# A sequence layer with routed experts on one core: TensorE transposes the identity where it would wait, and ScalarE takes the next group's first layer norm

## The reference, cut to what matters

```python
x = x + attn(_layernorm(x))      # in-projection, conv over 4 taps, damped oscillator scan, gate, out-projection
x = x + ffn(_layernorm(x))       # shared expert + 8 routed experts (top 2), exact gelu
def _layernorm(x, axis=-1, eps=1e-05):
    m = jnp.mean(x, axis=axis, keepdims=True)
    v = jnp.var(x, axis=axis, keepdims=True)
    return (x - m) / jnp.sqrt(v + eps)
# the scan, per head (64 wide, state 128):
v = (v - dt*A*y + dt*u*Bv) / denom;   y = y + dt*v + dt*u*By;   o = y.Cy + v.Cv
```

## Time and profile before

| | us |
|---|---|
| median of 3 runs (lowest, highest) | 561.17 (560.84, 562.13) |
| the profiled execution, its device time | 566.59 |
| its span, first to last instruction | 564.9 |
| PE busy | 456.9 (81%) |
| DVE busy | 454.3 (80%) |
| POOL busy | 283.8 (50%) |
| ACT busy | 238.8 (42%) |
| granted TensorE clock, mean | 0.921 |

### The profile page before, as it was taken

One profiled execution on the slowest core, in us unless ns is written; L12 is line 12 of the kernel. 1 busy time (PEld: TensorE's weight loads), 2 busy tenths in 40 slices (PEclk: granted clock), 3 DMA queues, 4 the chain that ended last, 5 costly groups with the idle time before them and its releaser, 6 DMA issues.

```text
span 564.9 us, 9434 instructions
## 1 busy us (share of the span) xinstructions
PE 456.9 (81%) x3163; PEld 352.7 (62%) x3163; DVE 454.3 (80%) x1280; ACT 238.8 (42%) x470; POOL 283.8 (50%) x361
## 2 busy tenths in 40 slices
PE   5882249993989959896689959898498996998997
PEld 4361248762856658674566747766385675786886
DVE  6599998968689997968689997977868987788542
ACT  1423225444275424443356523533437542443463
POOL 2007866666108855657305756576601785767100
PEclk9997569999899978999799995999899997998999
DMA  7400000200000010200000000020000000000000
GB/s 226 139 0 1 1 1 2 76 2 0 1 1 1 1 38 1 67 11 1 1 1 1 1 20 0 2 77 2 1 0 0 2 1 20 1 2 1 2 11 9
DMA packets 14793, 10.22 MB, mean 18 GB/s; under 512 B 1797, under 2 KB 13966, under 8 KB 14618
## 3 DMA queue, kind: packets, MB, share of 16 engines
q1 hardware_dynamic: 14746, 9.63, 5.9%
HBM read 8.55 MB, written 1.07 MB: 17 GB/s over the span
## 4 chain that ended last, share of the span: by engine, by line
DVE 37%; PE 36%; POOL 13%; issue 8%; ACT 4%; DMA 0%; SPq 0%; DVEq 0%; POOLq 0%; ACTq 0%
DVE tpA L1263 5%; PE BC L609 5%; DVE GV L1263 5%; DVE xr L1411 5%; PE HB L512 4%; POOL vt L1590 4%; PE HB L501 3%; DVE BC L1274 3%; POOL rinv L1625 3%; PE GV L631 3%; PE HB L569 3%; PE RR L667 2%; PE OO L684 2%; POOL big L1587 2%; DVE GV L1274 2%
## 5 line engine op out<-in xcount | busy, mean ns | idle before, releaser
L609 PE MATMUL BC<-xnT,winT 128*128 128x128 f32 x512 | 80.9, 309 | 44.2 <-DVE mm L1311 22.4
L609 PEld LDWEIGHTS BC<-xnT,winT 128*128 128x128 f32 x512 | 71.3, 216 | 57.4 <-issue 29.5
L1587 POOL TENSOR_TENSOR big<-mm 128x256 f32<-128x256 f32 x64 | 50.3, 785 | 74.7 <-DVE mm L1311 74.7
L1610 POOL TENSOR_SCALAR uT<-uT,skipT 128x512 f32<-128x512 f32 x8 | 12.5, 1570 | 95.4 <-DVE w L1396 55.5
L631 PE MATMUL GV<-big,vt 128*128 128x128 f32 x256 | 45.5, 305 | 17.6 <-POOL vt L1590 17.6
L1590 POOL TENSOR_TENSOR vt<-mm 128x256 f32<-128x256 f32 x64 | 58.5, 914 | 0.0
L561 PE MATMUL HB<-xnT,w 128*128 128x512 f32 x108 | 52.0, 603 | 3.7 <-ACT gtm L988 2.1
L631 PEld LDWEIGHTS GV<-big,vt 128*128 128x128 f32 x256 | 37.4, 210 | 23.4 <-POOL vt L1590 21.1
L1309 DVE TENSOR_TENSOR mm<-BC,pr 128x512 f32<-128x512 f32 x64 | 44.2, 691 | 6.0 <-DVE BC L1291 0.5
L925 ACT ACTIVATE big<-GV 128x256 f32<-128x256 f32 x60 | 23.0, 383 | 61.3 <-PE GV L634 59.6
L1599 POOL TENSOR_TENSOR mm<-ab,pr 128x256 f32<-128x256 f32 x48 | 41.4, 885 | 13.9 <-ACT pr L903 13.9
(11 more groups left out here) (208 smaller groups left out, 1133.8 us busy)
## 6 DMA issues: line engine op xcount, KB each, us to landing
ab<-dt_rows SPq DMA_DIRECT2D x12, 256.0 KB, 4.2
xr<-in_x SPq DMA_DIRECT2D x4, 256.0 KB, 5.1
winT<-in_w_inT SPq DMA_DIRECT2D x1, 1024.0 KB, 7.0
w<-in_rw SPq DMA_DIRECT2D x1, 1024.0 KB
out<-xr SPq DMA_DIRECT2D x3, 256.0 KB, 2.3
taps<-in_dw_wT SPq DMA_DIRECT2D x1, 512.0 KB, 3.7
w<-in_sw SPq DMA_DIRECT2D x2, 128.0 KB
out<-xr SPq DMA_DIRECT2D x2, 128.0 KB, 1.8
```

Of the source, the lines that this page charges most:

```text
L609: last = pe.matmul(b[:, j * TS:(j + 1) * TS], winT[:, col:col + NS], xt, start=True, stop=True)
L1587: pool.tensor_tensor(wt[q % 8][:], m[:, 0], m[:, 3], ALU.add)
```

## The change: what it does

Three things. `keep_busy` writes the HB bank that comes next instead of GV1, and therefore waits for the same read as that bank's next user. It is called in more places: more of them at the start (22, 3 and 15 for 10, 1 and 7); 5 after each of steps 14 to 31 of group 0; 3 after each of the first seven fills of every group and 4 more once DVE has scaled pair 0 (`first_pairs`, which also holds the two projections that open a group); 5 in `tail` of a group's last tile between its two products, 7 at the head of `op` of that tile, and 5 ahead of the second layer norm's transpose, for groups 0 to 2. And the first layer norm of groups 1 to 3 is applied by ACT (`Identity` with a scale and a bias, after pair 3's square and pair 1's copy) instead of DVE, for which POOL works out `shift` = -mean x rstd with two more small instructions.

```diff
-WARM = (10, 1, 7)
+WARM = (22, 3, 15)
+IDLE_STEP, PER_STEP, PER_FILL, AT_FIRST_PAIR = 14, 5, 3, 4
+AT_TAIL, AT_OUT, AT_NORM = 5, 7, 5
...
             def norm_T(kind, g):
+                if kind == LN2 and whole(g):
+                    keep_busy(AT_NORM)
                 pe.wait_ge(ln_xn, ln_index(kind, g) + 1)
...
             def keep_busy(n):
 
+                free = uses[0]
+                if free >= 2:
+                    pe.wait_ge(h_free, free - 1)
                 for _ in range(n):
-                    pe.transpose(GV[1][:, G_COLS], ident[:], ident[:])
+                    pe.transpose(HB[free % 2][:, 0:TS], ident[:], ident[:])
+
+            def first_pairs(g):
+
+                if g == 0:
+                    for i in range(IDLE_STEP, DS):
+                        pe.wait_ge(step, 3 * (i + 1))
+                        keep_busy(PER_STEP)
+                for q in range(2):
+                    proj(KP * g + q)
+                for n in range(1, FILL_OPS):
+                    pe.wait_ge(fill, FILL_OPS * g + n)
+                    keep_busy(PER_FILL)
+                pe.wait_ge(vc_done, KP * g + 1)
+                keep_busy(AT_FIRST_PAIR)
...
                     last.then_inc(r_done, 1)
+                if tile % GT == GT - 1 and tile < END:
+                    keep_busy(AT_TAIL)
                 pe.wait_ge(gm_done, NH * (tile + 1))
...
                 g, c = divmod(tile, GT)
+                if c == GT - 1 and tile < END:
+                    keep_busy(AT_OUT)
                 pe.wait_ge(skip_done, g + 1)
...
-                    for q in range(2):
-                        proj(KP * (g + 1) + q)
+                    first_pairs(g + 1)
...
             def front_early(g, k):
+                if g and k == F_XN:
+
+                    act.wait_ge(ln_rstd, ln_index(LN1, g) + 1)
+                    act.wait_ge(h_ready, USE[("xnT2", g - 2) if g >= 2 else ("xnT", g - 1)] + 1)
+                    for c in range(GT):
+                        last = act.activation(xn[:, c, :], xr[g % 3][:, c, :], ACT.Identity, bias=shift[:, c:c + 1],
+                                              scale=rstd[:, c:c + 1])
+                    last.then_inc(ln_xn, 1)
...
-                if k == F_XN:
+                if g == 0 and k == F_XN:
                     norm_apply(LN1, g)
...
+            def scale_and_shift(n):
+                pool.wait_ge(ln_var, n + 1)
+                pool.wait_ge(ln_xn, n)
+                pool.tensor_tensor(rstd[:], mv[:, :, 1], mhalf[:, 0:GT], ALU.pow)
+                link(pool.tensor_scalar(shift[:], mv[:, :, 0], -1.0, None, ALU.mult))
+                pool.tensor_tensor(shift[:], shift[:], rstd[:], ALU.mult).then_inc(ln_rstd, 1)
...
-                        rstd_of(ln_index(LN1, g + 1))
+                        scale_and_shift(ln_index(LN1, g + 1))
```

More of the change, by code:

```diff
@@ L148, in build @@
         rstd = sb("rstd", 128, GT)
+        shift = sb("shift", 128, GT)
         dtts = [sb(f"dtt{i}", 128, GT, 2, NH) for i in range(2)]
@@ L732, in _ @@
             pe.wait_ge(ab_done, 1)
-            for q in range(2):
-                proj(q)
+            first_pairs(0)
             for g in range(NG):
@@ L1090, in norm_stats @@
                     dve.wait_ge(ld_x[g], 16)
+                if ln_index(kind, u):
+                    dve.wait_ge(ln_xn, ln_index(kind, u))
                 for c in range(GT) if kind == LN1 else (c1 - 1,):
```

## The result

| | median us (lowest, highest) | runs |
|---|---|---|
| before | 561.38 (560.84, 562.89) | 6 |
| after | 570.35 (568.44, 573.05) | 6 |

The ratio is 1.016, interval 1.013 to 1.020: slower by 9 us. I had said slower, but 563.4, and the time lies just beyond my range of 556 to 570. Four executions of all that follow were disturbed (761 to 1470 us) and count in no ratio; the medians of three kernels count one each, which moves none by more than 0.2 us. The profiled execution after took 570.30 us, span 568.6, which is its median; PE is busy for 481.9 us (456.9 before), 42.7 of it with 281 turned identities, DVE for 447.6 (454.3 before).

A forecast was written before the change was run, and what follows sets the result against it. Neither PE nor DVE was taken to bound alone; group openings and ends mattered. Terms -1.8 - 1.4 + 1.9 + 0.3 + 5.6 - 2.3 = +2.3 on 566.59 gave 568.9, scaled 563.4 us; range 556 to 570.

The forecast's parts named there:

- the start-up: Start of the kernel: added transposes may raise the clock earlier, -1.8 us; bounds 0 and -4.5.
- the norm: Norm on ACT: +0.4 us in group 0; POOL's two instructions 0.5 us (bounds 0.3 and 1.0), ACT's four 1.1.
- the rests: Ends of groups 0 to 2: 51 transposes of 0.11 us where PE is the bound, +5.6 us; bounds 0 and +10.7.
- so I scale the result by 0.990: Whole kernel: the profiled 566.59 us is 1.0% over the median 561.17, so the sum's 568.9 became 563.4.
- the openings: Group openings: clock falls in PE's hole after pair 3's projection; group 0 +1.9 us, 1 and 2 -0.7 each, 3 +0.3.
- Given back ... -2.3: Whole kernel: delays ahead of a clock rise halve themselves, so half of 4.6 us returns, -2.3; bounds 0 and -4.6.
- my signs of being wrong: Wrong if the clock holds to the opening's end, PE idles beside the 17 transposes, or the clock stays low in fills.
- Steps of group 0: Matrix steps of group 0: five transposes a step raise the clock and then fit, delayed projections stay hidden; cost 0.
- Rival 3: Steps, fills, ends and openings: identity transposes do not count for the clock; 583.2 us, scaled 577.6; chance 0.05.
- Rival 1: Group openings: the clock holds through the hole too, perhaps removing the low stretch near 514; scaled 558.9 us; chance 0.22.
- Rival 2: Group ends: the 17 transposes find idle because the earlier chain shifts; 565.6 us, scaled 560.2; chance 0.10.
- rival 4: Whole kernel: it cancels, the delays being given back wholly at the next clock rise; 561.2 us; chance 0.11.

The follow-up runs named there:

- e12: The kernel before with the start-up's added transposes alone (22, 3, 15 instead of 10, 1, 7): 559.69 us, ratio 0.993 to before.
- e8: e2 with the first layer norm left on DVE, so start-up, step, fill and first-pair transposes only: 560.99 us, ratio 0.995 to before.
- e2: The changed kernel without the 17 transposes at the end of each of groups 0 to 2: 566.15 us, ratio 1.006 to before.
- e10: The whole changed kernel with POOL's ten small chunk-border instructions ahead of pair 0's product instead of pair 1's: 557.39 us, ratio 0.990 to before.
- e13: The kernel before with only the first layer norm of groups 1 to 3 moved to ACT and POOL: 567.74 us, ratio 1.006 to before.
- e14: e13 with POOL's ten small chunk-border instructions ahead of pair 0's product instead of pair 1's: 556.29 us, ratio 0.986 to before.
- e6: The kernel before with POOL's ten small chunk-border instructions ahead of pair 0's product instead of pair 1's: 557.69 us, ratio 0.990 to before.
- e7: e2 with POOL's ten small chunk-border instructions ahead of pair 0's product instead of pair 1's: 553.33 us, ratio 0.981 to before.
- e9: e8 with POOL's ten small chunk-border instructions ahead of pair 0's product instead of pair 1's: 552.70 us, ratio 0.981 to before.
- second recording of before: The kernel before, unchanged, profiled once more: the recorded execution took 565.62 us, against 566.59 in the first recording.
- e11: e2 with 24 identity transposes in PE's hole ahead of pair 1's product, POOL's product staying late: 559.11 us, ratio 0.991 to before.

## Why the prediction was wrong

The size failed, not the direction, and in three steps. Chained from kernel to kernel by their ratios to before (e12, e8, e2, after), the change is made up of -0.7% for the start-up, +0.2% for steps and fills, +1.0% for the norm and +1.1% for the rests: about -4, +1, +6 and +6 us. My sum had -1.8 for the start-up, 5.6 less 2.3 for the rests, and for the norm 0.4, in group 0 alone.

**"so I scale the result by 0.990".** On the recordings' own times the sum was nearly right: +2.3 forecast, 570.30 - 566.59 = +3.7 measured. But the 1% between recording and median was no factor that the changed kernel shares. The recording of before was one of the slow fifth of its executions; that of after was its median. Unscaled, the forecast would have been 568.9 for 570.35. The scaling took 5.5 us off that were not there, and hid that the usual execution of before is some 4 us quicker than the one I read, at the same mean clock. That the unscaled sum came so near is in part luck: nothing was given back where I had -2.3, the openings came to 0.0 for my +0.8, the end of group 3 was 1.1 us shorter for nothing, and the start-up gave 0.5 less.

**"Given back ... -2.3".** Little or nothing was given back. The three ends are longer by 1.4, 2.8 and 2.1 us, 6.3 in all for 5.6 forecast, and by 5.1 against e2, which lacks the 51 turns and nothing else; by the timed medians 4.2 (e2) and 4.1 (e10), by the ratios 6 and 5. Mechanism and place as said (no idle before any of them), and the low stretch at a group's end stayed.

**The norm, "+0.4" and "Bounds 0.3 and 1.0".** POOL's two instructions delayed it by 0.5 as said, from `rstd` at 208.22 to the crossings at 209.70 (1.48 us, and 0.99 in the kernel before, where only `rstd` stands there). ACT's four took 1.64 us, where I took 1.1 and bounded at 1.5. But its price is 3.6 to 5 us by the timed runs (e13's ratio and its median), 5.2 by e2 less e8, and nothing once POOL's product is early (-1.4 for e14 beside e6, +0.6 for e7 beside e9). So it is paid through the hole. Against the second recording of before, e13's is 4.0 us longer, all of it on the ways to pair 5 (0.7, 1.9 and 1.4 us in groups 0 to 2), and in group 1 with the clock low behind the hole for 6.8 us instead of 3.5. I had the hole in the openings' terms, as +1.9 against -2.6, and not as a price of the norm in the kernel as it usually runs.

**Openings.** Right on the recordings: group 0 +2.1 (forecast +1.9), groups 1 and 2 -1.1 and -0.8 (-0.7 each), group 3 -0.2 (+0.3). The clock fell after pair 3's projection as forecast in groups 0 to 2; e7 and e11 show that it needs the hole that POOL's late product leaves, and that a filled hole would have held the clock. One of my signs of being wrong came: in group 2 the clock stood at 0.50 through the fills (332.8 to 339.6), after PE had worked 2.36 of the 3.4 us before. The projections of the opening took 3.67 us there, and the turns were done with only at 342.6, without a price that the way to pair 5 shows (16.16 us, 15.96 in group 1).

**Start-up.** -1.3 for -1.8 in the recording, and 4 by the timed runs (e12), for which no stage accounts; the clock rose at 8.5 and was low under the 8-row products, the eight of which took 7.16 us again. Steps of group 0: 0, as forecast.

**Rival 3 and the rule of the Trainium skill.** Refuted. TensorE: Matmul & The Clock Gate, Part 4: PE-mode transpose, does not hold for these turns: between 56.3 and 59.7 us PE ran 18 of them and nothing else, and the clock went from 0.50 to 1.00; in e11, 24 of them stood in the hole, and it fell in none of the four, where in e2 it fell in three. **Rival 1** (the clock holds through the hole) fell with 83.6 and 213.3; its aside, that the low stretch near 514 may go, came true: group 3's end was 1.1 us shorter. **Rival 2** fell with the rests' rows, **rival 4** with the result.

What stays open: in which stage the usual execution of before, at 561 to 563, is shorter than its two recordings, and so where the start-up's four microseconds are won. Whether a recording itself favours the slow pattern in this kernel is open too; that e13's always fall badly is argued from one recording and from twelve times, of which three are under 566.

## What to carry to other kernels

Find out what PE waits for before filling its waits: here ten small GpSimd instructions, moved past one product, gave 5 to 13 us; turns of the identity paid in the start-up (4 us), in the steps and fills little even with the hole closed behind them (about 1 us), in the hole only to win back what the norm had cost, and never where PE is the bound. Before scaling one recording to a median, compare it with the spread of single runs: if it lies at an edge, the two kernels need not share the factor. A move whose direct price is half a microsecond can cost ten times as much where it lengthens an idle stretch ahead of dense PE work.

## What was not expected of the hardware

The same program shows different low stretches from run to run: group 1's opening at the low clock for 13.7 us in one recording, twice 3.4 in the other, with 1.4 us between their ways to pair 5, although the work of the pairs begins at the same time (pair 0 of group 0 at 74.90 and 74.91). A hole of 2.7 us ahead of pair 1's product brings the clock down in one group (213.3 after) and not in another (group 1 of e2). And the best opening is far better than any seen before: pair 5 after 12.4 us where the clock holds and POOL is early, 17.0 where neither does.
